# A message's scaling moved from VectorE to ScalarE and its constant to GpSimd, in the third edge stage of a four-layer graph network

## The chip, the cores and the metric

One core of a Trainium2 chip runs the whole program. The metric is device time in microseconds. The kernel before took 4991.14 us, the median of three runs (4990.61 to 4994.25).

## The reference, cut to what matters

The network has 3125 nodes, 103125 edges sorted by destination, and 64 features. Each of its four layers reads `h`, the rectified layer norm of the node rows, and adds its result to them. The change is in the third layer only, in the work done once per edge:

```python
def _mlp(x, ln_w, ln_b, W, b):
    h = _layer_norm(x, ln_w, ln_b)
    h = h @ W.T + b
    return leaky_relu(h, 0.01)
hn = _mlp(node_z, ...)            # 32 features per node
he = _mlp(edge_z, ...)            # 32 features per edge
msg = concatenate([hn[src], he])  # 64 features per edge
emb_edge = _mlp(msg, red_ln_w, red_ln_b, red_W, red_b)
msg_sum = segment_sum(emb_edge, dst) + emb_local
z = msg_sum / (deg + 1)
```

The layer norm's mean and weights are folded into the matrices beforehand. What is left per edge of the last `_mlp` is: multiply `msg` by two matrices (one gives the centred row, whose squares give the variance, the other gives the product), divide the product by the standard deviation, add the constant row `rc`, and take max(0.01 x, x). The division is a multiplication by a reciprocal, one number per edge. These three last steps are what the change redistributes.

## The kernel before, in words

Edges go in tiles of 128, one per partition, and eight tiles make a batch: there are 101 batches. Engines run their own in-order instruction lists and meet at semaphores. In `edge2` the batches come in groups of four; `q` and `h` give the place in the group (place = 2q + h, from 0 to 3). I call the stage's group "four places", and n the number of a batch, from 1.

Where the source rows `hn[src]` come from depends on the place. For places 0, 1 and 2 GpSimd gathers them with eight indirect DMAs per batch, one per tile (L950, in `Gather.gather`). For place 3 (`TAKEN`) there is no gather: TensorE picks the rows by 13 one-hot matmuls twice (`choose`, L1803), from one-hot matrices that VectorE writes (`hot`, L1947, 13 per group), and VectorE multiplies the outcome by a mask in two halves (`take`, L1957).

The order of the work of batch n is written out by hand on each engine:

- VectorE: `edge_row(n)` (L1963 to L1973: reciprocal, scale, constant, leaky relu of the edge part, which waits for ScalarE's `std1_ready`), the one-hot matrix of batch n-1 (L982), at place 3 the first `take`, then `add(n-2)`, eight additions to the accumulator (L1997) with up to five `hot` between them, at place 3 the second `take`, and last `message(n-1)`: reciprocal (L1979), scaling of eight tiles from PSUM (L1981), constant (L1984), leaky relu (L1987).
- TensorE: transposes of batch n (L1840; at place 3 L1812 and L1814), the edge matmuls of batch n+1 (L1787), then, after ScalarE has copied the transposes and VectorE has read the previous product (`u_sc`), the message matmuls of n (L1856), at place 2 the first `choose`, and the sums by destination of batch n-1 (L1795).
- ScalarE: copy of the transposes of n (L1899), eight squares and a root for the edge part of n+1 (L1876, L1880, `std1_ready`), the same for the message of n (`std2_ready`).
- GpSimd: the gathers, four batches ahead of their use. Besides waiting for the index list and for the buffer to be free, each half batch (four gathers) has a wait of its own in `midway`: at place 0 the second half waits for the sums of batch n-5, at place 1 the first half for the message matmuls of n-4 and the second for the transposes of n-3, at place 2 for sums of n-5 and message matmuls of n-3, n being the batch gathered.
- SyncE starts the loads of index lists, edge attributes and source numbers.

The buffers `u` and `u2` are single; the message product `rp`, in PSUM, is single too.

Of the kernel before, what the change touches and what calls it, by code (L numbers as in the profile page):

```python
# [203 lines left out]
def over(ap, n):  # L204

    return ap.unsqueeze(2).to_broadcast([ap.shape[0], ap.shape[1], n])
# [1471 lines left out]
def edge2(nc, k, cat, ga, catTp_ready):  # L1678


    with Ctx(nc, "edge2_") as c:
# [40 lines left out]
        by_bank = catTp[:, :, :].rearrange("p i e -> p (i e)")  # L1722
        row, ec, rc = fixed[:, 0:P].unsqueeze(1), fixed[:, P:P + HALF], fixed[:, 2 * P:2 * P + D]

        with nc.Block() as block:
# [37 lines left out]
            @block.gpsimd  # L1763
            def _(pool):
                def midway(pool, t, h, q, m, j):
                    if h == 1:
                        if j == 0:
# [7 lines left out]
                    elif q == 1:  # L1775
                        wait_past(pool, rp_ready, GROUP * (m - 1) + 4)
                ga.loop(nc, pool, begun=True, midway=midway)

# [93 lines left out]
            def _(act):  # L1872
# [17 lines left out]
                for i in (0, 1):  # L1890
                    act.activation(parts[:, :, i, 0, :], hn[:, i, :, :], ACT.Copy).then_inc(high_ready, 1)

                def body(t, first, last):
                    for h in (0, 1):
                        if empty(last, h):
                            continue
                        n = 2 * t + h + 1
                        act.wait_ge(catTp_ready, n + 2)
                        act.activation(catT[:, :, :], catTp[:, :, :], ACT.Copy).then_inc(catT_ready, 1)  # L1899
                        if not empty(last, h + 1):  # L1900
                            act.wait_ge(hep_ready, n + 1)
                            root(hep[:, :, HALF:HALF + D], 0, n + 1, sq1, std1_ready)
                        act.wait_ge(rp_ready, n)
                        root(rp[:, :, D:2 * D], 1, n, sq2, std2_ready)
                ends_apart(act, body)

            @block.vector
            def _(dve):
# [3 lines left out]
                dve.tensor_copy(ec, k.ec[:, :]).then_inc(row_ready, 1)  # L1912
                dve.tensor_copy(rc, k.rc[:, :]).then_inc(row_ready, 1)
                dve.memset(msg[0][:, :, D], 1.0)
                dve.memset(msg[1][:, :, D], 1.0).then_inc(ones_ready, 1)

                dve.wait_ge(row_ready, 3)
                step = Chain(dve, prep)
# [57 lines left out]

                def message(n, h):
                    dve.wait_ge(std2_ready, n)
                    dve.reciprocal(st[:, 5, :], st[:, 4, :]).then_inc(inv2, 1)  # L1979
                    dve.wait_ge(inv2, n)  # L1980
                    dve.tensor_tensor(u[:, :, :], rp[:, :, 0:D], over(st[:, 5, :], D),  # L1981
                                      ALU.mult).then_inc(u_sc, 1)
                    dve.wait_ge(u_sc, n)
                    dve.tensor_tensor(u2[:, :, :], u[:, :, :], rows_over(rc, B),  # L1984
                                      ALU.add).then_inc(u_b, 1)
                    dve.wait_ge(u_b, n)
# [27 lines left out]
                def body(t, q, m):  # L2014
                    first = isinstance(t, int) and t == 0
                    for h in (0, 1):
# [7 lines left out]
                        if b == TAKEN:  # L2024
                            take(m, 0)
                        if not first:
                            add(n - 2, h, t - 1, m + (b == TAKEN), due(t, m, b))
# [5 lines left out]
                        if not (first and h == 0):  # L2033
                            message(n - 1, 1 - h)
                by_parity(dve, body)
                onehot(dve, k, oh[0][:, :, :], PAIRS - 1, 0, row).then_inc(oh_ready, 1)
                add(USED - 1, 1, PAIRS - 2)
                message(USED, 0)
                add(USED, 0, PAIRS - 1)

# [766 lines left out]
```

## Time and profile before

| what | value |
|---|---|
| median of three runs | 4991.14 us |
| profiled execution, first to last instruction | 5820.0 us |
| profiled execution's own time beyond that span | none is given |
| stage of the change in it (first to last instruction, about) | 2520 to 3660 us |
| its steady part that is read below | 2560 to 3640 us |
| mean granted TensorE clock, whole span / steady part | 0.875 / 0.85 |

The profiled execution is 829 us, or 16.6%, longer than the median of the runs. The table of stretches in the rows below cuts the program into its parts (three edge stages, then the fourth edge stage in two passes, with short node stages between them); the line of the stage of the change is shown. A stretch's line gives the busy time of each engine with its number of instructions. An engine's time between instructions is given in the groups as idle time with what ended it.

### The profile page before, as it was taken

Reading aid. Unit: us, or ns where it says so; the run is one execution under the profiler, and the core shown is the slowest. Engines: PE = TensorE matmul, PEld = TensorE weight load, DVE = VectorE, ACT = ScalarE, POOL = GpSimd, SP = SyncE. Lnnn points to the kernel's source line nnn. Section 1 sums busy time; section 2 is a strip of 40 time slices with the busy share of each in tenths; the row PEclk is TensorE's granted clock in tenths of the full one; section 3 lists DMA queues with packets and bytes.
Section 4 is the critical chain, followed back from the end, with each engine's and each line's share of the span. In section 5 each row is a group of like instructions: output and inputs, shape, how many; then the busy total and the mean of one; then the engine's idle time right before and its main releaser. Section 6 shows DMA issues by size and latency. Waiting matters only on the chain. (4 is left out here: it accounts for less than half of the span.)

```text
span 5820.0 us, 104938 instructions
## 1 busy us (share of the span) xinstructions
PE 4388.1 (75%) x29528; PEld 2834.6 (49%) x29528; DVE 4126.9 (71%) x7954; ACT 2011.5 (35%) x6556; POOL 3270.2 (56%) x2950
## 2 busy tenths in 40 slices
PE   2999899989677777756777777376777667549998
PEld 1444444444344444445555555244444434349998
DVE  4767676766777676767777777466666666789998
ACT  2656566666000000134434444000000000057775
POOL 4666666663566666455555554455555555325554
PEclk6999999999788888778888888688888888779998
DMA  4333333331212111121111111233333333211111
GB/s 114 91 90 94 87 87 93 94 87 48 52 43 44 40 43 44 23 47 45 45 42 47 44 45 35 63 101 103 100 103 101 105 106 102 78 43 47 49 49 33
DMA packets 493105, 394.00 MB, mean 68 GB/s; under 512 B 346007, under 2 KB 379168, under 8 KB 492904
## 3 DMA queue, kind: packets, MB, share of 16 engines
q1 hardware_dynamic: 395496, 303.53, 18.3%
q0 software_dynamic: 90560, 83.37, 8.0%
q10 hardware_dynamic: 6976, 6.23, 0.3%
q8 instruction: 34, 0.56, 0.0%
q14 instruction: 39, 0.32, 0.0%
HBM read 355.34 MB, written 37.42 MB: 67 GB/s over the span
## 5 line engine op out<-in xcount | busy, mean ns | idle before, releaser
L1093 POOL DMA_INDIRECT edge_src_rows<-table_wh,edge_gather_idx x806 | 867.8, 1077 | 503.0 <-issue 229.7
L950 POOL DMA_INDIRECT edge3a_src_rows<-table_h,edge3a_gather_idx x808 | 763.1, 944 | 632.7 <-issue 259.0
L2165 PE MATMUL edge3a_z_ps<-Wz,edge3a_both_ends_t 128*128 128x396 f32 x1616 | 736.3, 600 | 405.0 <-DVE edge3a_terms L2258 322.0
L1123 PE MATMUL edge_sums_ps<-edge_onehot_src,edge_halves 128*128 128x512 bf16 x4840 | 890.0, 331 | 43.2 <-issue 32.4
L950 POOL DMA_INDIRECT table_cat<-table_hn,table_gather_idx x592 | 624.9, 1056 | 479.6 <-PE edge_sums_ps L1795 181.2
L1508 POOL DMA_INDIRECT edge_src_rows<-table_h,edge_gather_idx x608 | 609.1, 1002 | 424.4 <-issue 175.4
L2258 DVE SCALAR_TENSOR_TENSOR edge3a_terms<-edge3a_z_ps,att_z 128x792 f32<-128x792 f32 x404 | 386.1, 977 | 486.6 <-DMA edge_edge_attr<-in_ea 307.5
L2165 PEld LDWEIGHTS edge3a_z_ps<-Wz,edge3a_both_ends_t 128*128 128x128 f32 x1616 | 346.6, 226 | 733.7 <-DVE edge3a_terms L2258 368.3
L1123 PEld LDWEIGHTS edge_sums_ps<-edge_onehot_src,edge_halves 128*128 128x128 f16 x4840 | 385.6, 97 | 477.4 <-issue 69.5
L2577 PE MATMUL edge3b_sums_ps<-edge3b_onehot,edge3b_weighted 128*128 128x128 f32 x4848 | 572.9, 279 | 6.3 <-DVE layers_accT L2615 4.4
L2577 PEld LDWEIGHTS edge3b_sums_ps<-edge3b_onehot,edge3b_weighted 128*128 128x128 f32 x4848 | 553.6, 193 | 12.0 <-DVE layers_accT L2615 4.6
L2494 POOL TENSOR_TENSOR edge3b_weighted<-edge3b_src_rows,edge3b_alpha 128x1920 f32<-128x1920 f32 x101 | 350.2, 3468 | 345.4 <-DVE edge3b_alpha L2594 251.4
L2204 ACT ACTIVATE edge3a_both_ends_t<-edge3a_both_ends_t_ps 128x1024 f32<-128x1024 f32 x101 | 103.4, 1024 | 1245.3 <-DMA edge_edge_attr<-in_ea 992.0
L2543 ACT ACTIVATE edge3b_weighted<-edge3b_src_rows,edge3b_alpha 128x64 f32<-128x64 f32 x1818 | 445.2, 334 | 166.2 <-DVE edge3b_alpha L2594 157.4
L1523 PE MATMUL edge_src_rows_t_ps<-edge_onehot_src,edge_h_halves 128*128 128x512 f16 x1300 | 364.2, 415 | 142.3 <-DVE edge_onehot_src L1629 75.3
L1211 DVE TENSOR_SCALAR edge_onehot_src<-layer_node_row,edge_src_col,edge_magnitude 128x1568 bf16<-128x1568 f16 x605 | 416.9, 690 | 26.0 <-remote 18.1
L1301 DVE TENSOR_TENSOR edge_halves<-edge_weighted_ps,edge_halves 128x512 f16<-128x512 f32 x204 | 131.0, 683 | 345.9 <-ACT edge_halves L1172 266.7
L2266 DVE TENSOR_REDUCE edge3a_scores<-edge3a_terms 128x24 f32<-128x1584 f32 x202 | 364.5, 1805 | 6.9
L1123 PE MATMUL edge_sums_ps<-edge_onehot_src_act,edge_halves 128*128 128x512 bf16 x1608 | 307.3, 330 | 60.2 <-issue 40.0
L1164 ACT ACTIVATE edge_onehot_src_act<-edge_distance,edge_magnitude,edge_minus_magnitude 128x1568 bf16<-128x1568 f16 x201 | 340.5, 1694 | 10.5
L1629 DVE TENSOR_SCALAR edge_onehot_src<-edge_src_everywhere,node_col 128x1024 f16<-128x1024 f16 x650 | 333.0, 516 | 9.2
L1593 ACT ACTIVATE edge_msg<-edge_msg_ps 128x512 f32<-128x512 f32 x101 | 60.3, 597 | 791.2 <-remote 451.6
(370 smaller groups left out, 7950.6 us busy)
## 6 DMA issues: line engine op xcount, KB each, us to landing
edge_dst_row<-in_dst_row SPq DMA_DIRECT2D x102, 512.0 KB
edge3a_dst_row<-in_dst_row SPq DMA_DIRECT2D x102, 512.0 KB
edge_window<-table_wh_parts SPq DMA_DIRECT2D x816, 48.8 KB
edge3a_window<-table_h SPq DMA_DIRECT2D x816, 32.0 KB
edge_edge_attr<-in_ea SPq DMA_DIRECT2D x101, 256.0 KB
kept_rows<-edge3a_src_rows SPq DMA_DIRECT2D x101, 256.0 KB
edge3b_src_rows<-kept_rows SPq DMA_DIRECT2D x101, 256.0 KB
edge_edge_attr<-in_ea SPq DMA_DIRECT2D x101, 128.0 KB
```

The source lines that it names most:

```text
L950: nc.gpsimd.indirect_dma_start(self.slot(b, j), None, self.table[:, :], bass.IndirectOffsetOnAxis(ap=self.idx[b][:, j:j + 1], axis=0)).the ...
L1093: nc.gpsimd.indirect_dma_start(g[q][:, j, :], None, k.t_wh[:, :], bass.IndirectOffsetOnAxis(ap=idx[q][:, j:j + 1], axis=0)).then_inc(gathe ...
L1123: mm = pe.matmul(acc[:, i, 0:w], halves[q][:, j, a, :, :].rearrange("p h d -> p (h d)"), hot[:, o:o + w], start=first and a == 0, stop=False)
L1211: dve.tensor_scalar(slot_v(q, j)[:, :], k.node_row[:, :], col[q][:, j:j + 1], mag[q][:, j:j + 1], ALU.is_equal, ALU.mult).then_inc(hot_v, 1)
L1508: nc.gpsimd.indirect_dma_start(g[p][:, j, :], None, k.t_h[:, :], bass.IndirectOffsetOnAxis(ap=idx[p][:, j:j + 1], axis=0)).then_inc(gather ...
L1523: mm = pe.matmul(rowsTp[:, o:o + 512], h16[:, b, :], ring[b % RING][:, o:o + 512], start=(b == 0), stop=(b == NB - 1))
L2165: mm = pe.matmul(zp[q % 2][:, i, 0:H * ZH], hcT[h][:, j * P:(j + 1) * P], k.Wz[:, :], start=True, stop=True)
L2258: dve.scalar_tensor_tensor(terms[:, 2 * q:2 * q + 2, :], zp[q % 2][:, :, 0:H * ZH], 0.0, rows_over(k.att_z[:, :], 2), ALU.max, ALU.mult).t ...
L2266: dve.tensor_reduce(scs[h][:, :, j:j + B // 2].rearrange("p h b -> p b h"), terms[:, j:j + B // 2, :].rearrange("p b (h f) -> p b h f", h= ...
L2494: return engine.tensor_tensor(hp[h][:, a:b, :, :], rows, weights, ALU.mult)
L2543: w = act.activation(hp[h][:, j, a, :], st[h][:, j, :], ACT.Copy, scale=al[h][:, a, j:j + 1])
L2577: mm = pe.matmul(sums[j % 4][:, i, :], hp[h][:, j, 2 * i:2 * i + 2, :].rearrange("p a d -> p (a d)"), oh[h][:, j, :], start=True, stop=True)
```

## The change

VectorE keeps the reciprocal (`invert`) and the leaky relu (`finish`). The reciprocal now comes before `add`, and the leaky relu stays where `message` was. ScalarE scales the product tile by tile, eight activations of 128x64 from PSUM with the reciprocal as scale, at the head of the next batch's body, ahead of the copy of the transposes. GpSimd adds the constant row with one operation of 128x512, read from SBUF: at places 0 to 2 in the middle of a batch's eight gathers, ahead of the second half's own wait, at place 3 by itself. The constant's copy in PSUM goes.

```diff
             @block.gpsimd
+                def shift(n):
+                    pool.wait_ge(u_sc, n)
+                    nc.gpsimd.tensor_tensor(u2[:, :, :], u[:, :, :], rows_over(k.rc[:, :], B),
+                                            ALU.add).then_inc(u_b, 1)
                 def midway(pool, t, h, q, m, j):
+                    if j and live_shift(t, h):
+                        shift(2 * t + h - 3)
                     if h == 1:
...
-                ga.loop(nc, pool, begun=True, midway=midway)
+                def live_shift(t, h):
+                    return not isinstance(t, int) or 2 * t + h >= 4
+                def body(t, q, m):
+                    if isinstance(t, int) and t == 0:
+                        return
+                    for h in (0, 1):
+                        if not used_batch(t, h):
+                            continue
+                        ga.gather(nc, pool, t, h, q, m, midway=midway)
+                        if 2 * q + h == TAKEN and live_shift(t, h):
+                            shift(2 * t + h - 3)
+                by_parity(pool, body)
+                for n in range(USED - 3, USED + 1):
+                    shift(n)
             @block.scalar
+                def scale(n):
+                    act.wait_ge(inv2, n)
+                    wait_past(act, u_b, n - 1)
+                    for j in range(B):
+                        a = act.activation(u[:, j, :], rp[:, j, 0:D], ACT.Copy, scale=st[:, 5, j:j + 1])
+                    a.then_inc(u_sc, 1)
                 def body(t, first, last):
                         n = 2 * t + h + 1
+                        if not (first and h == 0):
+                            scale(n - 1)
                         act.wait_ge(catTp_ready, n + 2)
...
+                scale(USED)
             @block.vector
-                dve.tensor_copy(rc, k.rc[:, :]).then_inc(row_ready, 1)
...
-                def message(n, h):
+                def invert(n):
                     dve.wait_ge(std2_ready, n)
                     dve.reciprocal(st[:, 5, :], st[:, 4, :]).then_inc(inv2, 1)
-                    dve.wait_ge(inv2, n)
-                    dve.tensor_tensor(u[:, :, :], rp[:, :, 0:D], over(st[:, 5, :], D),
-                                      ALU.mult).then_inc(u_sc, 1)
-                    dve.wait_ge(u_sc, n)
-                    dve.tensor_tensor(u2[:, :, :], u[:, :, :], rows_over(rc, B),
-                                      ALU.add).then_inc(u_b, 1)
+                def finish(n, h):
                     dve.wait_ge(u_b, n)
                     dve.scalar_tensor_tensor(msg[h][:, :, 0:D], u2[:, :, :], 0.01, u2[:, :, :],
                                              ALU.mult, ALU.max).then_inc(msg_ready, 1)
...
+                        if not (first and h == 0):
+                            invert(n - 1)
                         if not first:
                             add(n - 2, h, t - 1, m + (b == TAKEN), due(t, m, b))
...
-                            message(n - 1, 1 - h)
+                            finish(n - 1, 1 - h)
```

## Rows read from the trace of the kernel before

**Rows 1.** The head of the profile's page: span, then busy time of each engine.

```profile
span 5820.0 us, 104938 instructions
## 1 busy us (share of the span) xinstructions
PE 4388.1 (75%) x29528; PEld 2834.6 (49%) x29528; DVE 4126.9 (71%) x7954; ACT 2011.5 (35%) x6556; POOL 3270.2 (56%) x2950
```

**Rows 2.** The table of stretches, the line of this stage; columns head it.

```profile
core 0: us, PE busy (x) PEld busy (x) DVE busy (x) ACT busy (x) POOL busy (x), PEclk, DMA share, GB/s
...
2520.00:3660.00 1140.00, 790.62 (x6056) 611.09 (x6056) 826.78 (x2208) 465.13 (x3538) 624.92 (x592) 0.84 0.18 44
```

**Rows 3.** The scalings' line: count, shortest/median/longest ns, first and last start.

```profile
L1981 DVE TENSOR_TENSOR edge_u<-edge_msg_ps,edge_stat x101: 690/692/693, 2547.8 to 3651.8; 128x512 f32<-128x512 f32 x101
```

**Rows 4.** The same table for the stage's steady part alone.

```profile
2560.00:3640.00 1080.00, 760.86 (x5852) 585.94 (x5853) 790.56 (x2110) 447.19 (x3417) 602.54 (x569) 0.85 0.18 43
```

**Rows 5.** Who waited for whom in the steady part: us in total, times, longest.

```profile
ACT edge_squares L1876 <- DMA edge_edge_attr<-in_ea: 215.6, 38, 9.4
DVE edge_stat L1963 <- ACT edge_stat L1880: 182.1, 57, 8.5
...
PE edge_msg_ps L1856 <- DVE edge_u L1981: 165.0, 55, 4.6
```

**Rows 6.** VectorE in order of time, one group: start, length, [idle before].

```profile
2787.10 0.20 DVE L1963 RECIPROCAL edge_stat<-edge_stat 128x8 f32<-128x8 f32 x1 [8.24 <-ACT edge_stat L1880]
...
2790.96 0.62 DVE L1947 TENSOR_SCALAR edge_onehot_src<-edge_src_in_half,edge_node_no 128x1024 f16<-128x1024 f16 x1 [0.29 <-PE edge_cat_t_ps L1803]
...
2798.98 0.20 DVE L1963 RECIPROCAL edge_stat<-edge_stat 128x8 f32<-128x8 f32 x1 [1.91 <-ACT edge_stat L1880]
...
2801.67 0.28 DVE L1997 TENSOR_TENSOR layers_accT<-layers_accT,edge_sums_ps 65x128 f32 x1
...
2809.74 0.20 DVE L1963 RECIPROCAL edge_stat<-edge_stat 128x8 f32<-128x8 f32 x1 [2.11 <-ACT edge_stat L1880]
...
2817.92 0.20 DVE L1963 RECIPROCAL edge_stat<-edge_stat 128x8 f32<-128x8 f32 x1
...
2824.69 0.69 DVE L1987 SCALAR_TENSOR_TENSOR edge_msg<-edge_u 128x512 f32<-128x512 f32 x1
2833.11 0.20 DVE L1963 RECIPROCAL edge_stat<-edge_stat 128x8 f32<-128x8 f32 x1 [7.72 <-ACT edge_stat L1880]
```

**Rows 7.** TensorE in order of time, third batch of that group.

```profile
2821.64 1.14 PE L1787 MATMUL edge_he_ps<-eR,edge_edge_attr 64*128 64x96 f32 x16
```

**Rows 8.** ScalarE in order of time, third batch of that group.

```profile
2830.99 0.22 ACT L1876 ACTIVATE edge_squares<-edge_he_ps 128x64 f32<-128x64 f32 x1 [8.03 <-DMA edge_edge_attr<-in_ea]
...
2832.77 0.30 ACT L1880 ACTIVATE edge_stat<-edge_stat,eps 128x8 f32<-128x8 f32 x1
```

**Rows 9.** Groups of instructions of VectorE, steady part, shapes apart; columns head it.

```profile
line engine op names shapes xcount | busy us, mean ns | idle before us <-releasers
...
L1987 DVE SCALAR_TENSOR_TENSOR edge_msg<-edge_u 128x512 f32<-128x512 f32 x97 | 67.5, 695 | 3.4
L1981 DVE TENSOR_TENSOR edge_u<-edge_msg_ps,edge_stat 128x512 f32<-128x512 f32 x97 | 67.1, 692 | 3.3
L1984 DVE TENSOR_TENSOR edge_u<-edge_u,edge_constants_ps 128x512 f32<-128x512 f32 x97 | 66.6, 686 | 3.3
...
L1979 DVE RECIPROCAL edge_stat<-edge_stat 128x8 f32<-128x8 f32 x97 | 18.5, 191 | 0.0
```

**Rows 10.** Groups of ScalarE in the second pass of the fourth stage.

```profile
L2543 ACT ACTIVATE edge3b_weighted<-edge3b_src_rows,edge3b_alpha 128x64 f32<-128x64 f32 x1818 | 445.2, 334 | 166.2 <-DVE edge3b_alpha L2594 157.4 <-DMA edge3b_src_rows<-kept_rows 8.8
```

**Rows 11.** Groups of ScalarE in the steady part.

```profile
L1899 ACT ACTIVATE edge_cat_t<-edge_cat_t_ps 128x512 f32<-128x512 f32 x97 | 57.5, 593 | 255.1 <-PE edge_cat_t_ps L1814 122.6 <-issue 79.8 <-DMA edge_gather_idx<-in_src_t 35.3
```

**Rows 12.** GpSimd's groups over the whole span.

```profile
L950 POOL DMA_INDIRECT edge3a_src_rows<-table_h,edge3a_gather_idx x808 | 763.1, 944 | 632.7 <-issue 259.0 <-DMA kept_rows<-edge3a_src_rows 165.5 <-DMA edge_edge_attr<-in_ea 137.7
...
L2494 POOL TENSOR_TENSOR edge3b_weighted<-edge3b_src_rows,edge3b_alpha 128x1920 f32<-128x1920 f32 x101 | 350.2, 3468 | 345.4 <-DVE edge3b_alpha L2594 251.4 <-DMA edge3b_src_rows<-kept_rows 94.0
...
L854 POOL TENSOR_TENSOR node_heads<-layers_accT,layer_accT 128x256 f32<-128x256 f32 x1 | 2.4, 2426 | 0.0
```

**Rows 13.** GpSimd's groups in the steady part.

```profile
L950 POOL DMA_INDIRECT table_cat<-table_hn,table_gather_idx x569 | 602.5, 1059 | 458.2 <-PE edge_sums_ps L1795 181.2 <-issue 153.2 <-PE edge_msg_ps L1856 106.7
```

**Rows 14.** GpSimd's waits in the steady part: us in total, times, longest.

```profile
POOL table_cat L950 <- PE edge_sums_ps L1795: 181.2, 47, 7.7
POOL table_cat L950 <- issue: 153.2, 470, 2.0
POOL table_cat L950 <- PE edge_msg_ps L1856: 106.7, 41, 8.3
```

**Rows 15.** GpSimd in order of time, two gathers of the group above.

```profile
2790.39 0.94 POOL L950 DMA_INDIRECT table_cat<-table_hn,table_gather_idx  x1 [6.97 <-PE edge_sums_ps L1795]
2791.64 1.98 POOL L950 DMA_INDIRECT table_cat<-table_hn,table_gather_idx  x1 [0.30 <-issue]
```

More of the change, by code:

```diff
@@ L1722, in edge2 @@
         by_bank = catTp[:, :, :].rearrange("p i e -> p (i e)")
-        row, ec, rc = fixed[:, 0:P].unsqueeze(1), fixed[:, P:P + HALF], fixed[:, 2 * P:2 * P + D]
+        row, ec = fixed[:, 0:P].unsqueeze(1), fixed[:, P:P + HALF]
         with nc.Block() as block:
@@ L1912, in _ @@
                 dve.tensor_copy(ec, k.ec[:, :]).then_inc(row_ready, 1)
-                dve.tensor_copy(rc, k.rc[:, :]).then_inc(row_ready, 1)
                 dve.memset(msg[0][:, :, D], 1.0)
                 dve.memset(msg[1][:, :, D], 1.0).then_inc(ones_ready, 1)
-                dve.wait_ge(row_ready, 3)
+                dve.wait_ge(row_ready, 2)
                 step = Chain(dve, prep)
@@ L2033, in body @@
                         if not (first and h == 0):
-                            message(n - 1, 1 - h)
+                            finish(n - 1, 1 - h)
                 by_parity(dve, body)
                 onehot(dve, k, oh[0][:, :, :], PAIRS - 1, 0, row).then_inc(oh_ready, 1)
+                invert(USED)
                 add(USED - 1, 1, PAIRS - 2)
-                message(USED, 0)
+                finish(USED, 0)
                 add(USED, 0, PAIRS - 1)
```

## The prediction

> **What bounds the kernel now.** I read the head of the page, the table of stretches, the waits of the stage, and one group of four batches in order of time. The page says that no engine is full: TensorE is busy 75%, VectorE 71%, GpSimd 56% [rows 1]. The table of stretches puts the stage of the change at 2520 to 3660 us [rows 2]; 101 batches in it are 25.25 groups, and I use 1105 us for them, from the first scaling at 2547.8 to the last at 3651.8 [rows 3], or 43.8 us a group. In its steady part VectorE is busy 790.6 of 1080 us, GpSimd 602.5, ScalarE 447.2 [rows 4].
>
> The waits are where the reader must be careful. ScalarE waits 215.6 us for something to square, and VectorE 182.1 us for ScalarE's root [rows 5]. In the group in order of time VectorE starts batches at 2787.10, 2798.98, 2809.74, 2817.92 and 2833.11, so places 3, 0, 1 and 2 take 11.88, 10.76, 8.18 and 15.19 us [rows 6]. The 15.19 hold an idle time of 7.72. TensorE's record of the matmuls that ScalarE needs next ends at 2821.64 + 1.14 = 2822.78 [rows 7]; ScalarE starts on them at 2830.99, having been idle 8.03 [rows 8]. The records show nothing in those eight microseconds that it needed. The same, smaller, lies before 2809.74. I take these two pauses as belonging to the profiled execution only, because that execution is 829 us longer than the median of the runs (5820.0 [rows 1] against 4991.14) and the time must be somewhere. That is a choice, and a rival below drops it.
>
> Without them a group takes 11.88 + (10.76 - 2.11) + 8.18 + (15.19 - 7.72) = 36.2 us [rows 6], 914 us for the stage. In 36.2 us VectorE idles only some 2 or 3: in the timed runs **VectorE's order bounds the stage now**, at place 3 joined by TensorE's picking.
>
> **What the change does, part by part.** My sum is for one group, times 25.25. It is made on the records of the profiled execution less the two pauses, and its difference is then added to the median of 4991.14.
>
> *VectorE, removed.* Scaling and constant, 0.692 and 0.686 us each as single instructions [rows 9], follow each other every 0.72: 1.44 us a batch. At places 0 to 2 this is on the path; at place 3 VectorE idles 1.91 us afterwards for ScalarE [rows 6], and it is hidden. VectorE alone would then need 8.65 - 1.44 = 7.2, 6.7 and 6.0 us there. The one reciprocal is moved, not removed: 0.19 us [rows 9]. The copy of the constant at the start is 64 columns, once: nothing.
>
> *TensorE, a wait shortened.* The message matmuls wait for the scaling in 55 batches, 165.0 us [rows 5], since `add` stood before it. That wait now ends earlier. What is late next is ScalarE's copy of the transposes.
>
> *ScalarE, added.* Eight activations a batch with a scale of one number per partition. The like row is that of 128x64 activations with such a scale: 445.2 us for 1818, 0.245 each, 0.334 for a lone one [rows 10]. So 7 x 0.245 + 0.334 = 2.05 us. The source is PSUM there and SBUF in the row; the squares read PSUM and come no slower. Bounds: 1.6 us (the step of the squares without that scale: 2830.99 to 2832.77 is 1.78 with the last one's end [rows 8]) and 8 x 0.334 = 2.7. ScalarE is busy 447.2 of 1080 [rows 4], so it has the time, but its place is at the head of the body, and what is queued behind it is the copy, the squares and the root that VectorE's next batch waits for. This makes a loop. From VectorE's first reciprocal of a batch: edge part and one-hot matrix to 2801.67, 2.69 us after 2798.98 [rows 6]; reciprocal and handing over 0.24; scaling 2.05; copy 0.59 [rows 11] and handing over 0.06; squares and root, from the first square to VectorE's next reciprocal, 2833.11 - 2830.99 = 2.12 [rows 6, 8]. Sum 7.75. So places 0 to 2 cannot fall to VectorE's 7.2, 6.7 and 6.0, but to 7.75 each; place 2 even grows from 7.47. Place 3 stays at 11.88, its scaling lying beside TensorE's picking. A group by this loop: 3 x 7.75 + 11.88 = 35.1.
>
> *GpSimd, added.* One addition of 128x512 a batch. The nearest like row is the 128x1920 product, 3.468 us [rows 12]; in proportion 0.925, and I take 1.0, and 0.1 for starting it. Below, 0.93; above, the 128x256 addition of the last node stage, 2.43 [rows 12], which reads with a permuted step, so that I hold it for the far end. GpSimd's own work: 24 gathers a group, mean 1.059 us [rows 13], each with a gap of 153.2 / 470 = 0.326 [rows 14]: 24 x 1.385 = 33.2 us. With four additions, 33.2 + 4 x 1.1 = **37.6 us**. This is more than the 36.2 of now and the 35.1 of ScalarE's loop.
>
> Its slack is what pays today: it waits 181.2 and 106.7 us for TensorE [rows 14], most of it in the profiled pauses. Without them it has 36.2 - 33.2 = 3.0 us a group, and gets 4.4 of work. *The wait added:* `shift` waits for ScalarE's scaling; queued behind it are the second half of a batch's gathers and all later ones; TensorE's transposes four batches on wait for these. And the other way: VectorE's `finish`, and behind it the next edge part, wait for the addition; so does ScalarE's next scaling, since `u` is single, and behind that the copy and the root. GpSimd running late thus stops all four engines. SyncE's index loads wait for the gathers, as before, one group ahead.
>
> *Two rules weighed.* The trace's gathers take 0.944 in the first pass of the fourth stage [rows 12] and 1.059 here [rows 13]; one that started at 2791.64 took 1.98 while VectorE wrote one-hot matrices [rows 6, 15]. The Trainium skill (SBUF — State Buffer, Who interferes with whom) says that VectorE's fast two-port operations and GpSimd exclude each other for a whole instruction. By that rule, which these rows agree with, an addition that meets `hot` costs one of the two up to the other's length; at 0.3 us a meeting it would be four times 0.3, 1.2 us a group, 30 us more. No row shows an addition meeting one, and it is not in my sum. The Trainium skill (GPSIMD Engine Reference, Performance versus the Vector engine) gives some 2.6 cycles an element for a two-input addition and advises VectorE for it; an estimate from that page is 1.1 us for 512 elements beside the row's 0.925, 10 us more over the stage.
>
> **The sum.** 37.6 - 36.2 = +1.4 us a group, x 25.25 = +35. Start and end of the stage add a last addition and its handing over, 1 us. 4991 + 36 = **5027 us**, slower by 0.7%.
>
> **Rivals.**
>
> *GpSimd does not bind; the kernel gets faster.* If the 0.326 gap between gathers is partly the profiler's, GpSimd's 37.6 shrinks: it decides below a gap of (35.1 - 4.4 - 24 x 1.059) / 24 = 0.22. Then the group is ScalarE's 35.1: -1.1 x 25.25 = -28, **4963 us**. For it: the whole execution is slowed by profiling. Against it: the gap is the same 0.30 in all gathers, whatever surrounds them. Chance 0.18.
>
> *The two pauses are real.* Then GpSimd has 43.8 - 37.6 = 6 us to spare. Place 1 goes from 8.18 to 7.75, place 2 in the groups without a pause does not gain, and what TensorE's shortened wait gives is at most the 1.44 us of place 0: 0.4 to 1.8 a group, 10 to 45 us, **4970 us**. For it: nothing in the records separates a real wait from a profiled one. Against it: the 829 us. Chance 0.10.
>
> *The addition's wait stops the gathers.* At place 0 the second half waited for sums that were there; now it waits for the scaling, ready 2.69 + 0.24 + 2.05 = 5.0 us into the next batch, while the first half (4 x 1.385 = 5.5 us, started with the transposes at 2.3) ends at 7.8, the batch's own end. So up to 5.0 us of idle a group where GpSimd is on time, none where it is late by them. As it binds, I take half: 2.5 x 25.25 = +63 on top, **5090 us**; an addition of 1.7 us in place of 1.0 gives the same. Chance 0.22.
>
> *The edits cancel*: GpSimd's 37.6 overlaps the slow places so that 36.2 stays, within 10 us of **4991**. Chance 0.14.
>
> My forecast has 0.36. This kernel's measurement tells 0.2%, 10 us, from no change. Faster: 0.18 + 0.10 = 0.28. Same: 0.14. Slower: 0.36 + 0.22 = 0.58. The range goes from 4950, which takes in both faster rivals' values, to 5100; the forecast's own is 5005 to 5050. The far ends of the addition's price (2.43 us: +1.4 x 101 = 141 more) lie outside.
>
> **What would show it.** After, the addition's group should say about 1.0 us x 101; the scaling's 808 activations 0.25 each. GpSimd's waits for TensorE should be nearly gone in unpaused groups, with short ones for ScalarE's scaling in their place, and VectorE should wait for GpSimd before L1987's successor, which it never does now. TensorE's 165.0 us for L1981 should have no successor of that size. The profiled span may even shrink where the pauses remain, since there GpSimd has room; the timed median is what my sum is about. I am wrong if GpSimd still idles 2 us or more a group in unpaused groups, if the addition takes over 1.5 us, or if the stage gets shorter in the timed runs.

## The result, and the profile after

The changed kernel takes **5033.26 us** (median, 5029.01 to 5033.79), the kernel before 4990.88 in runs beside it (4988.85 to 4994.25): slower by 0.81%, ratio 1.0081, 95% interval 1.0068 to 1.0094. The forecast was 5027.

The head of the page after, as [rows 1]:

```profile
span 5031.9 us, 105710 instructions
## 1 busy us (share of the span) xinstructions
PE 4094.4 (81%) x29353; PEld 2742.8 (55%) x29528; DVE 4021.6 (80%) x7751; ACT 2176.0 (43%) x7364; POOL 3411.7 (68%) x3051
```

The span is 5031.9 us, beside runs of 5033: this profile shows the kernel as it runs when timed. That of [rows 1] did not (5820.0 beside 4991), so the kernel before was profiled once more. From here "before" means that second profile (it stands as an experiment below), and group lengths are counted as the first to the last batch of the stage over 25 groups of four batches.

The stretch from 2300 to 3150 us, first after and then before, columns as in [rows 2]:

```profile
2300.00:3150.00 850.00, 622.78 (x5192) 482.25 (x5191) 612.01 (x1709) 531.94 (x3706) 680.95 (x605) 0.90 0.22 50
```

```profile
2300.00:3150.00 850.00, 647.55 (x5431) 522.38 (x5432) 736.99 (x1975) 420.77 (x3177) 571.27 (x537) 0.87 0.21 51
```

VectorE lost 125 us of work in the same 850 us, GpSimd got 110 more. The granted TensorE clock of this stretch is 0.90 after and 0.87 before, so the loss is not a lower clock. Next the one-line summaries (count; shortest, median, longest ns; first and last start), of the new addition and scaling after, and of the old scaling before, which answers to [rows 3]:

```profile
L1767 POOL TENSOR_TENSOR edge_u<-edge_u,rc x101: 1260/1274/1668, 2223.4 to 3200.8; 128x512 f32<-128x512 f32 x101
```

```profile
L1919 ACT ACTIVATE edge_u<-edge_msg_ps,edge_stat x808: 304/328/360, 2221.6 to 3200.4; 128x64 f32<-128x64 f32 x162
```

```profile
L1981 DVE TENSOR_TENSOR edge_u<-edge_msg_ps,edge_stat x101: 690/692/692, 2236.0 to 3170.0; 128x512 f32<-128x512 f32 x101
```

The addition and the old scaling each come once a batch, so their first and last starts give the stage: 977.4 us after, 934.0 before, **39.1 and 37.4 us a group**. The stage's 43 us are the whole loss of 42. (The profiled spans differ by 31 only: the second profile of the kernel before took 5002 us, 11 more than its median, and its stage starts 14 us later, at 2236.0 against 2221.6.)

GpSimd's groups after (busy us, mean ns, idle before and its releasers), as [rows 13]:

```profile
L950 POOL DMA_INDIRECT table_cat<-table_hn,table_gather_idx x519 | 567.8, 1094 | 147.7 <-issue 143.8 <-PE edge_sums_ps L1817 2.7 <-PE edge_msg_ps L1878 0.3
L1767 POOL TENSOR_TENSOR edge_u<-edge_u,rc 128x512 f32<-128x512 f32 x86 | 113.7, 1323 | 21.6 <-ACT edge_u L1919 20.5
```

Add up: 567.8 + 113.7 busy, 143.8 of the fixed gaps between gathers, 23.5 of all waits, together 849 of 850 us. GpSimd had 115 us of waits for TensorE in the kernel before and has 3.0 now; it never rests. That it sets the pace is what the experiments test. One group is 24 x (1.094 + 143.8 / 519) + 4 x 1.323 = 32.9 + 5.3 = 38.2, plus waits of 0.9 for ScalarE's scaling: 39.1, the measured length.

The waits after on VectorE, as [rows 5] (total, times, longest):

```profile
DVE edge_msg L2014 <- POOL edge_u L1767: 214.6, 53, 6.1
...
DVE edge_stat L1994 <- ACT edge_stat L1902: 4.1, 9, 1.0
```

VectorE now waits 214.6 us for GpSimd's addition, a wait that did not exist, and hardly at all for ScalarE's root (4.1 us). TensorE's wait for the scaling (165.0 us in [rows 5]) has no successor; in its place stands what was named as late next, ScalarE's copy:

```profile
PE edge_msg_ps L1878 <- ACT edge_cat_t L1930: 79.8, 68, 1.9
```

How the addition arrives late is seen in one group in order of time (start, length, [idle before]), first GpSimd, as [rows 15]:

```profile
2578.12 1.64 POOL L1767 TENSOR_TENSOR edge_u<-edge_u,rc 128x512 f32<-128x512 f32 x1 [1.15 <-ACT edge_u L1919]
2579.91 1.41 POOL L950 DMA_INDIRECT table_cat<-table_hn,table_gather_idx  x1
...
2589.11 0.94 POOL L950 DMA_INDIRECT table_cat<-table_hn,table_gather_idx  x1 [0.30 <-issue]
2590.07 1.27 POOL L1767 TENSOR_TENSOR edge_u<-edge_u,rc 128x512 f32<-128x512 f32 x1
2591.50 1.40 POOL L950 DMA_INDIRECT table_cat<-table_hn,table_gather_idx  x1 [0.16 <-issue]
...
2602.70 1.27 POOL L1767 TENSOR_TENSOR edge_u<-edge_u,rc 128x512 f32<-128x512 f32 x1
...
2608.42 1.98 POOL L950 DMA_INDIRECT table_cat<-table_hn,table_gather_idx  x1 [0.30 <-issue]
2610.42 1.27 POOL L1767 TENSOR_TENSOR edge_u<-edge_u,rc 128x512 f32<-128x512 f32 x1
...
2617.86 1.60 POOL L1767 TENSOR_TENSOR edge_u<-edge_u,rc 128x512 f32<-128x512 f32 x1 [0.52 <-ACT edge_u L1919]
```

and VectorE, as [rows 6]:

```profile
2578.15 0.48 DVE L1978 TENSOR_SCALAR edge_onehot_src<-edge_src_in_half,edge_node_no 128x1024 f16<-128x1024 f16 x1
...
2579.80 0.69 DVE L2014 SCALAR_TENSOR_TENSOR edge_msg<-edge_u 128x512 f32<-128x512 f32 x1 [0.34 <-POOL edge_u L1767]
...
2583.52 0.20 DVE L2010 RECIPROCAL edge_stat<-edge_stat 128x8 f32<-128x8 f32 x1
...
2591.38 0.69 DVE L2014 SCALAR_TENSOR_TENSOR edge_msg<-edge_u 128x512 f32<-128x512 f32 x1 [5.82 <-POOL edge_u L1767]
...
2604.00 0.69 DVE L2014 SCALAR_TENSOR_TENSOR edge_msg<-edge_u 128x512 f32<-128x512 f32 x1 [4.46 <-POOL edge_u L1767]
...
2609.66 0.47 DVE L1978 TENSOR_SCALAR edge_onehot_src<-edge_src_in_half,edge_node_no 128x1024 f16<-128x1024 f16 x1
...
2610.26 1.72 DVE L1978 TENSOR_SCALAR edge_onehot_src<-edge_src_in_half,edge_node_no 128x1024 f16<-128x1024 f16 x1
...
2612.52 0.68 DVE L2014 SCALAR_TENSOR_TENSOR edge_msg<-edge_u 128x512 f32<-128x512 f32 x1
```

and ScalarE's eight scalings between them, merged into one line:

```profile
2583.83 1.75 ACT L1919 ACTIVATE edge_u<-edge_msg_ps,edge_stat 128x64 f32<-128x64 f32 x8 [1.07 <-DVE edge_stat L2010]
```

VectorE hands over its reciprocal at 2583.72 (2583.52 + 0.20), and ScalarE has scaled by 2585.58. GpSimd starts the addition only at 2590.07, 4.5 us later, since it stands behind eight gathers that began at 2579.91. VectorE gets its message at 2591.38 after 5.82 us of idling. The second thing to see is at 2610: a one-hot write that takes 0.47 us takes 1.72 when it meets the addition of 2610.42, and the addition of 2578.12 takes 1.64 instead of 1.27 beside the write of 2578.15. The two hold each other up.

VectorE's one-hot writes after and before (columns as in [rows 9]):

```profile
L1978 DVE TENSOR_SCALAR edge_onehot_src<-edge_src_in_half,edge_node_no 128x1024 f16<-128x1024 f16 x281 | 172.6, 614 | 4.9 <-PE edge_cat_t_ps L1825 4.9
```

```profile
L1947 DVE TENSOR_SCALAR edge_onehot_src<-edge_src_in_half,edge_node_no 128x1024 f16<-128x1024 f16 x293 | 139.0, 474 | 0.0
```

Their mean went from 474 to 614 ns: 13 writes a group (293 in 850 us), 1.8 us.

### The profile page after: what moved, and what is told of

Read it like the earlier page. It is cut to its first block and busy times, and to the rows that moved or that the text cites. A ratio compares the mean times of both kernels' runs of the same rounds, so it can differ in the third digit from the quotient of the medians.

```text
span 5031.9 us, 105710 instructions
## 1 busy us (share of the span) xinstructions
PE 4094.4 (81%) x29353; PEld 2742.8 (55%) x29528; DVE 4021.6 (80%) x7751; ACT 2176.0 (43%) x7364; POOL 3411.7 (68%) x3051
## 5 line engine op out<-in xcount | busy, mean ns | idle before, releaser
L1093 POOL DMA_INDIRECT edge_src_rows<-table_wh,edge_gather_idx x806 | 852.0, 1057 | 332.8 <-issue 255.2
L1123 PE MATMUL edge_sums_ps<-edge_onehot_src,edge_halves 128*128 128x512 bf16 (+1 forms) x4689 | 857.3, 327 | 23.1 <-DVE edge_onehot_src L1211 14.6
L950 POOL DMA_INDIRECT table_cat<-table_hn,table_gather_idx x592 | 647.0, 1093 | 180.3 <-issue 164.8
L2195 PE MATMUL edge3a_z_ps<-Wz,edge3a_both_ends_t 128*128 128x396 f32 x1616 | 583.3, 512 | 10.1 <-DVE edge3a_terms L2288 8.5
L2573 ACT ACTIVATE edge3b_weighted<-edge3b_src_rows,edge3b_alpha 128x64 f32<-128x64 f32 x1818 | 445.2, 334 | 165.5 <-DVE edge3b_alpha L2624 156.6
L2195 PEld LDWEIGHTS edge3a_z_ps<-Wz,edge3a_both_ends_t 128*128 128x128 f32 x1616 | 292.9, 191 | 257.0 <-DVE edge3a_terms L2288 76.9
L2186 PE MATMUL edge3a_both_ends_t_ps<-edge3a_onehot_t,edge3a_window 128*64 128x128 f32 x1616 | 223.7, 298 | 213.6 <-DMA edge3a_src_rows<-table_h,edge3a_gather_idx 213.4
L1817 PE MATMUL edge_sums_ps<-edge_onehot,edge_msg 128*65 128x128 f32 x1616 | 246.7, 318 | 140.3 <-issue 77.8
L2186 PEld LDWEIGHTS edge3a_both_ends_t_ps<-edge3a_onehot_t,edge3a_window 128*64 128x64 f32 x1616 | 198.2, 150 | 275.2 <-issue 178.3
```

What stands on the lines that cost most here:

```text
L950: nc.gpsimd.indirect_dma_start(self.slot(b, j), None, self.table[:, :], bass.IndirectOffsetOnAxis(ap=self.idx[b][:, j:j + 1], axis=0)).the ...
L1093: nc.gpsimd.indirect_dma_start(g[q][:, j, :], None, k.t_wh[:, :], bass.IndirectOffsetOnAxis(ap=idx[q][:, j:j + 1], axis=0)).then_inc(gathe ...
L1123: mm = pe.matmul(acc[:, i, 0:w], halves[q][:, j, a, :, :].rearrange("p h d -> p (h d)"), hot[:, o:o + w], start=first and a == 0, stop=False)
L2186: pe.matmul(hcTp[D:P, cols], win[h][:, j, :], oht[h][:, cols], start=True, stop=True)
L2195: mm = pe.matmul(zp[q % 2][:, i, 0:H * ZH], hcT[h][:, j * P:(j + 1) * P], k.Wz[:, :], start=True, stop=True)
L2573: w = act.activation(hp[h][:, j, a, :], st[h][:, j, :], ACT.Copy, scale=al[h][:, a, j:j + 1])
```

## The experiments

All ratios are to the kernel before, in runs on the same chip, with 95% intervals (its medians there lie between 4990 and 4995 us); "group" is the stage's length per four batches. Diffs are against the changed kernel.

**The kernel before, once more** (no edit). It was to say whether the two pauses in [rows 6] are the kernel's.

> The kernel before, profiled once more. The profile of the changed kernel spans 5031.9 us and its median is 5033.3, so that execution shows nearly the timed run; the one of before spans 5820.0 against 4991. If the pauses of 2.1 and 7.7 us in a group belong to that one profiled execution, this profile spans about 4990, a group of four batches takes 36 to 37 us (the prediction's 36.2), VectorE idles 2 to 3 us in it, and GpSimd waits 3 to 4 us in it. If they are real, the span is again above 5400 and a group takes 43 to 44.

One run took 5002.31 us, the profiled span is 5000.5, the group 37.4. The waits:

```profile
PE edge_msg_ps L1856 <- DVE edge_u L1981: 169.3, 67, 3.9
POOL table_cat L950 <- issue: 143.9, 439, 1.5
...
POOL table_cat L950 <- PE edge_sums_ps L1795: 81.1, 35, 3.0
...
DVE edge_stat L1963 <- ACT edge_stat L1880: 44.7, 27, 1.9
DVE layers_accT L1997 <- PE edge_sums_ps L1795: 43.3, 52, 0.9
POOL table_cat L950 <- PE edge_msg_ps L1856: 34.3, 35, 1.6
```

VectorE's wait for the root fell from 182.1 us, longest 8.5, to 44.7, longest 1.9. The pauses are not in the kernel; the choice to take them out was right. The other expectations were missed a little: a group takes 37.4 us and not 36 to 37, VectorE waits 88 us for others (3.9 a group, not 2 to 3), and GpSimd 115 (5.1 a group, not 3 to 4). VectorE is busy 737 of 850 us: its order is read as the bound.

**The constant back on VectorE** (const_on_vector). The scaling stays on ScalarE; GpSimd gets nothing.

```diff
                 def shift(n):
-                    pool.wait_ge(u_sc, n)
-                    nc.gpsimd.tensor_tensor(u2[:, :, :], u[:, :, :], rows_over(k.rc[:, :], B),
-                                            ALU.add).then_inc(u_b, 1)
+                    pass
...
                 def finish(n, h):
+                    dve.wait_ge(u_sc, n)
+                    dve.tensor_tensor(u2[:, :, :], u[:, :, :], rows_over(rc, B),
+                                      ALU.add).then_inc(u_b, 1)
```

> The changed kernel, with the constant added by VectorE again (before the leaky relu, 0.69 us a batch), ScalarE's scaling kept where it is. Theory (GpSimd's list is full: 24 gathers of 1.37 us and four additions of 1.32, 38.2 of the 39.3 us that a group takes): GpSimd has 33 us of work again and stops binding; the places 0 to 2 take VectorE's 7.9, or ScalarE's loop of 7.75, and a group 35 to 36 us: 4960 to 4985 us, under both kernels. Rival (ScalarE's scaling ahead of the copy is what made it slower): the loop is unchanged, and so is the time, 5020 to 5035.

4953.34 us, ratio 0.9917 (0.9904 to 0.993), group 35.7; 7 us under the expected range. The half of the change that goes to ScalarE is worth 40 us (4993.37 for the kernel before beside it); the half that goes to GpSimd costs 80 on top of it. The one-hot writes are back at 486 ns. The ScalarE half also puts the reciprocal ahead of `add`, and no run moves VectorE's own scaling there with the constant left on VectorE; so how much of the 40 us is the engine and how much the earlier place is open.

**The scaling back on VectorE** (scale_on_vector). The other half alone; `scale` goes from ScalarE's body (not shown).

```diff
                 def invert(n):
                     dve.reciprocal(st[:, 5, :], st[:, 4, :]).then_inc(inv2, 1)
+                    dve.wait_ge(inv2, n)
+                    wait_past(dve, u_b, n - 1)
+                    dve.tensor_tensor(u[:, :, :], rp[:, :, 0:D], over(st[:, 5, :], D),
+                                      ALU.mult).then_inc(u_sc, 1)
```

> The changed kernel with the scaling done by VectorE in one operation, right behind its reciprocal and ahead of the additions to the accumulator; the constant stays on GpSimd. ScalarE is as before the change. Theory (GpSimd's list is full): the same 38.2 us of GpSimd's work in a group, so 5020 to 5040 us, no faster than the changed kernel by more than 10. Rival (ScalarE's loop): it is gone, VectorE has 0.69 us less than before the change on its path, and the time falls under 4985.

5045.4 us, 1.0103 (1.0088 to 1.0117), group 39.5; 5 us over the expected range. GpSimd's constant alone costs 52 us, all of the loss and more. Its groups:

```profile
L950 POOL DMA_INDIRECT table_cat<-table_hn,table_gather_idx x511 | 548.7, 1074 | 161.2 <-issue 136.1 <-PE edge_msg_ps L1878 22.9
L1767 POOL TENSOR_TENSOR edge_u<-edge_u,rc 128x512 f32<-128x512 f32 x85 | 108.2, 1273 | 32.6 <-DVE edge_u L2010 31.6
```

24 x (1.074 + 0.266) + 4 x 1.273 is 37.3, and its waits of 54.5 us in 21.5 groups are 2.5: 39.8, near the measured 39.5. These waits are longer than the changed kernel's 0.9.

**The addition twice** (double_addition), the first time into a buffer that nobody reads, to price one addition.

```diff
+                    nc.gpsimd.tensor_tensor(u3[:, :, :], u[:, :, :], rows_over(k.rc[:, :], B), ALU.add)
                     nc.gpsimd.tensor_tensor(u2[:, :, :], u[:, :, :], rows_over(k.rc[:, :], B),
```

> The changed kernel, with GpSimd's addition done twice a batch, the first into a buffer that nobody reads. Theory (GpSimd's list is full, so each microsecond on it is one of the stage's): 101 more additions of 1.32 us are 133 us, so 5033 + 133 = 5166, between 5150 and 5185. Rival (it is the places of the waits that cost, GpSimd has slack): well under that, below 5120.

5157.75 us, 1.0332 (1.0316 to 1.0348), group 44.0. That is 124 us over the changed kernel, for 101 additions of 1.30 = 131: nearly each microsecond given to GpSimd lengthens the kernel.

**Two columns of 64** (two_columns): the wait and its place stay, the work all but goes.

```diff
-                    nc.gpsimd.tensor_tensor(u2[:, :, :], u[:, :, :], rows_over(k.rc[:, :], B),
+                    nc.gpsimd.tensor_tensor(u2[:, :, 0:2], u[:, :, 0:2], rows_over(k.rc[:, 0:2], B),
...
+                dve.memset(u2[:, :, :], 0.0)
```

> The changed kernel with all its waits, but GpSimd adds the constant to 2 of 64 columns of each tile alone, the others of the buffer being zero from the start: 128x16 in place of 128x512. Theory (the length of the addition fills GpSimd's list): four additions of about 0.2 in place of 1.32 us leave 34 us of GpSimd's work in a group; VectorE stops waiting for it and the time falls to 4950 to 4985. Rival (it is the place of the additions: each stands behind up to eight gathers, and each stops the gathers behind it until ScalarE has scaled): the waits stay, and the time stays above 5015.

4958.7 us, 0.9921 (0.9901 to 0.9941). The six runs lie apart, three from 4942 to 4948 and three from 4970 to 4975; the profile, with a group of 36.6, is of the longest.

```profile
L1767 POOL TENSOR_TENSOR edge_u<-edge_u,rc x101: 215/228/689, 2229.1 to 3143.3; 128x16 f32<-128x16 f32 x101
```

The addition takes 0.228 us (median; mean 0.297 in the 850 us). 75 us are gone by the medians, 58 to 91 by single runs, though VectorE still waits 130.6 us for GpSimd (46 times, longest 4.1) behind the gathers: the work on GpSimd's list is most of the loss, and it was wrong to expect VectorE's waits to end. VectorE has one instruction of 0.69 less a batch than in const_on_vector (4953), and by the medians is no faster. That the late arrival eats this saving fits the waits, but the spread of the runs is too wide to show it.

**The scaling behind ScalarE's copy** (scale_behind_copy), in the changed kernel.

```diff
-                        if not (first and h == 0):
-                            scale(n - 1)
                         act.wait_ge(catTp_ready, n + 2)
                         act.activation(catT[:, :, :], catTp[:, :, :], ACT.Copy).then_inc(catT_ready, 1)
+                        if not (first and h == 0):
+                            scale(n - 1)
```

> The changed kernel, with ScalarE's scaling behind its copy of the transposes and ahead of the squares. Theory (GpSimd's list is full): ScalarE's order decides nothing, 5025 to 5045. Rival (ScalarE's loop has a share): 10 us or more either way.

5088.51 us, 1.0193 (1.0178 to 1.0209), group 41.0: no change was expected, and it is 55 us slower than the changed kernel. The waits:

```profile
DVE edge_msg L2014 <- POOL edge_u L1767: 276.9, 82, 6.5
ACT edge_cat_t L1928 <- PE edge_cat_t_ps L1836: 243.2, 20, 13.3
...
PE edge_msg_ps L1878 <- ACT edge_u L1919: 132.5, 83, 2.4
```

At place 3 the copy waits for TensorE's picking, up to 13.3 us; the scaling is now queued behind that, and GpSimd and VectorE behind the scaling. GpSimd waits 54.4 us in 20.7 groups, 2.6 a group in place of 0.9.

**The same order, with the constant on VectorE** (const_on_vector_copy_first), the edits of const_on_vector and scale_behind_copy together.

> The kernel with the constant on VectorE and the scaling on ScalarE (4953 us), with the scaling behind the copy of the transposes. There GpSimd does not bind; the loop over ScalarE's list and VectorE's own list are within 0.2 us a batch of each other. The loop has the same length in either order if the copy does not wait, and gains up to the copy's 0.6 us where the copy was ready and the reciprocal was not: TensorE waits 100.7 us for the copy there. If the loop binds places 0 to 2: 4925 to 4945. If VectorE's own list binds: 4945 to 4960.

4993.37 us, 1.0 (0.9991 to 1.0009), group 37.4: 40 us over const_on_vector, and outside both expected ranges. The same cause (the copy waits 182.3 us, longest 9.2; VectorE 92.6 us for the scaling) without GpSimd in it. The place of the scaling at the head of the body, which the prediction took as given, is needed for the whole gain of ScalarE's half.

**The constant on GpSimd for place 3's message alone** (const_split): const_on_vector with one batch in four on GpSimd.

```diff
-                def finish(n, h):
+                def finish(n, h, by_pool=False):
+                    if not by_pool:
+                        dve.wait_ge(u_sc, n)
+                        dve.tensor_tensor(u2[:, :, :], u[:, :, :], rows_over(rc, B),
+                                          ALU.add).then_inc(u_b, 1)
...
-                            finish(n - 1, 1 - h)
+                            finish(n - 1, 1 - h, b == 0)
```

> The kernel with scaling on ScalarE, the constant on VectorE at three places of four, and on GpSimd for the message of place 3, where GpSimd has no gather. GpSimd then has 33 + 1.3 = 34.3 us of work in a group of 35.7. If a place on the list is all that counts, VectorE gains 0.69 us in one batch of four: 17 us, 4936. If the addition, met by VectorE's writing of one-hot matrices, makes these wait, the gain is lost: 4950 to 4965.

4976.23 us, 0.9964 (0.9951 to 0.9978), group 36.5: 23 us worse than leaving it on VectorE, and over both expected ranges. VectorE waits 1.5 us in all for GpSimd, so it is not lateness. It is mostly the one-hot writes, VectorE's line in this kernel:

```profile
L1976 DVE TENSOR_SCALAR edge_onehot_src<-edge_src_in_half,edge_node_no 128x1024 f16<-128x1024 f16 x290 | 170.4, 587 | 0.0
```

587 ns against 486: 13 x 0.10 = 1.3 us a group, for 0.69 saved, a net 0.6 of the 0.8 that a group grew. Place by place the traces agree: place 0, where the addition falls, takes 8.50 us against 7.97 in const_on_vector, its five writes 3.77 against 2.51; the other 0.2 us lies at place 3 and is open.

**The same where no one-hot write runs** (const_split_quiet): place 1's message, finished in place 2's body; `b == 0` above becomes `b == 2`, and GpSimd's addition stands in place 1's second half.

> As the split kernel (4976 us), but the message whose constant GpSimd adds is that of place 1, which VectorE finishes in the body of place 2, where it writes no one-hot matrices for the picking. In the split kernel these writes rose from 0.486 to 0.587 us, 13 of them 1.3 us a group, more than the 0.69 that VectorE saves. Theory (the addition on GpSimd and VectorE's two-speed writes shut each other out): the mean write stays at 0.49, VectorE's 0.69 stay saved, and the time comes under the 4953 of the kernel with the constant on VectorE, or within 5 us of it, for the body of place 2 is bound by ScalarE's loop: 4935 to 4960. Rival (any addition on GpSimd costs by the wait behind its four gathers): 4970 or more.

4973.82 us, 0.9958 (0.9945 to 0.9971), group 36.6. The writes are back at 487 ns, as expected, and yet nothing is gained: the time is in the rival's range, not the theory's; GpSimd and VectorE in order of time:

```profile
2600.57 0.94 POOL L950 DMA_INDIRECT table_cat<-table_hn,table_gather_idx  x1 [0.30 <-issue]
2601.54 1.27 POOL L1767 TENSOR_TENSOR edge_u<-edge_u,rc 128x512 f32<-128x512 f32 x1
2602.97 1.40 POOL L950 DMA_INDIRECT table_cat<-table_hn,table_gather_idx  x1 [0.16 <-issue]
```

```profile
2597.67 0.20 DVE L2008 RECIPROCAL edge_stat<-edge_stat 128x8 f32<-128x8 f32 x1
...
2602.85 0.69 DVE L2016 SCALAR_TENSOR_TENSOR edge_msg<-edge_u 128x512 f32<-128x512 f32 x1 [3.13 <-POOL edge_u L1767]
```

The addition comes 3.7 us after the reciprocal's end, behind the gathers that stand ahead of it, and VectorE idles 3.13 for it (75.4 us, 23 times). Place 2, where this falls, takes 8.66 us against 7.25 in const_on_vector, and place 3 gets back 0.7 of it. So one cost was exchanged for the other, and both are seen in the trace.

**The additions in other places** (additions_spread): in the changed kernel, behind the 4th, 10th, 16th and 22nd gather of a group.

```diff
-                    if j and live_shift(t, h):
+                    if live_shift(t, h) and (h == 0 and q == 0 and j == 4 or h == 1 and j == 2 or q == 1 and j == 0):
                         shift(2 * t + h - 3)
+                    if q == 1 and j == 6 and live_shift(t, h + 1):
+                        shift(2 * t + h - 2)
```

> The changed kernel with the four additions of a group behind the 4th, 10th, 16th and 22nd of its 24 gathers, in place of the 4th, 12th, 20th and 24th; the gathers' own waits are where they were. GpSimd's work is the same: 24 x 1.37 + 4 x 1.32 = 38.2 us a group, of the 39.1 that a group takes. Theory (the total binds): between 38.2 and 39.1 us a group, 5010 to 5035 us. Rival (the uneven distance of the additions is most of the loss: VectorE waits up to 6.1 us for the late ones): 5000 or less.

5015.65 us, 1.0041 (1.0029 to 1.0053), group 38.2.

```profile
L950 POOL DMA_INDIRECT table_cat<-table_hn,table_gather_idx x533 | 587.2, 1102 | 149.5 <-issue 149.2 <-PE edge_msg_ps L1880 0.3
L1767 POOL TENSOR_TENSOR edge_u<-edge_u,rc 128x512 f32<-128x512 f32 x89 | 113.5, 1276 | 1.6
```

GpSimd hardly waits now (0.3 us for TensorE), and its list is 24 x (1.102 + 0.280) + 4 x 1.276 = 38.3, the measured group to 0.1. The changed kernel's other 0.9 us a group is the wait for the scaling.

**The second reciprocal first** (early_inverse: the changed kernel; const_on_vector_early_inverse: with the constant on VectorE). ScalarE waited 220.6 us for that reciprocal after the change; it stood behind the one-hot matrix of 1.21 us, and at place 3 behind the first `take`.

```profile
ACT edge_u L1919 <- DVE edge_stat L2010: 220.6, 87, 5.8
```

```diff
+                            invert(n - 1)
...
-                        if not (first and h == 0):
-                            invert(n - 1)
```

> The changed kernel (constant on GpSimd) with the same single step that took 39 us off the kernel with the constant on VectorE: the reciprocal ahead of the one-hot matrix, so that ScalarE scales 0.7 us or more earlier in each batch. Theory (GpSimd's list is full): GpSimd waits for the scaling 20.5 us in 86 additions, that is all it can win: 5015 to 5033. Rival (ScalarE's loop is what binds here as well): 39 us or so off, 5000 or less.

> The kernel with the constant on VectorE and the scaling on ScalarE, and VectorE's reciprocal ahead of the one-hot matrix of the batch before. The loop by ScalarE's list, from root to root, loses the one-hot matrix's 1.13 us less a wait of some 0.4 for the second root: VectorE waits 95 us for that root now, 57 times. If the loop binds there, half or more of these go: 4900 to 4935 us. If VectorE's own list binds, the new wait costs as much as it gives: 4945 to 4965.

early_inverse takes 5006.78 us, 1.003 (1.002 to 1.0041), group 37.9. GpSimd's lines:

```profile
L950 POOL DMA_INDIRECT table_cat<-table_hn,table_gather_idx x532 | 580.5, 1091 | 149.0 <-issue 146.3 <-PE edge_cat_t_ps L1862 1.2 <-PE edge_sums_ps L1817 0.3
L1767 POOL TENSOR_TENSOR edge_u<-edge_u,rc 128x512 f32<-128x512 f32 x89 | 113.8, 1278 | 4.2 <-ACT edge_u L1919 1.9
```

Its wait for the scaling goes from 20.5 to 1.9 us, the additions' mean from 1.323 to 1.278; the list is 24 x (1.091 + 146.3 / 532) + 4 x 1.278 = 37.9, again the measured group. The gain of 26 us is more than the wait that was to be all it could win, and the time is 8 us under the expected range: of the 1.2 us a group, 0.9 is the wait, 0.2 the additions and 0.1 the gathers. **const_on_vector_early_inverse takes 4914.62 us**, 0.9836 (0.9823 to 0.9849), group 34.1, and beats both kernels. The same edit is worth 26 us where GpSimd is the bound and 39 where it is not.

## Why the prediction was right

*What bounds before.* Right: VectorE's order. The group was put at 36.2 us from the records less the pauses, and is 37.4; VectorE idles 88 us of 850 for ScalarE's root and TensorE's sums, 3.9 a group, where "some 2 or 3" had been read. From the first scaling to the last are 25 groups, not 25.25; this is worth 0.4 us in the 43.8, and nothing in the forecast.

*VectorE and TensorE.* As described: 1.44 us a batch gone, and ScalarE's copy late next.

*ScalarE.* The size of one term was off: eight scalings take 1.75 us, not 2.05. The loop's 35.1 us a group cannot be seen alone; const_on_vector, where VectorE keeps 0.69 us a batch, has 35.7. In the changed kernel it does not bind. What the loop's reading did not see is that one part of it could go: the 1.2 us that the reciprocal stands behind the one-hot matrix.

*GpSimd.* The step that carried the forecast, and it is shown: a list of 24 gathers and four additions that sets the pace (double_addition lengthens the kernel by nearly what it adds, and the list's sum is the measured group in additions_spread and early_inverse). Forecast 33.2 + 4.4 = 37.6; measured 32.9 for the gathers, 5.3 for the additions, 0.9 of waits, 39.1. The mis-sized term is the addition, 1.323 us on average where 1.0 and a start of 0.1 had been taken from the 128x1920 product in proportion to its columns [rows 12]. The estimate from the Trainium skill (GPSIMD Engine Reference, Performance versus the Vector engine), 1.1 us, was nearer than the row's 0.925, and its advice to leave such an addition to VectorE is borne out: const_on_vector is 80 us faster than the changed kernel.

*The difference.* Forecast +1.4 us a group, measured 39.1 - 37.4 = +1.7, times 25: +43, against +35. Both lengths had been read too short, by 1.5 and 1.2; most of the two errors cancel, and 5027 against 5033 looks better than its terms. Part of this is luck. In the kernel before GpSimd's list is 24 x (1.064 + 143.9 / 537) = 32.0 us, so its slack was 5.4 and not 3.0; what came on top was 5.3 of additions, 0.9 of dearer gathers and 0.9 of waits, 7.1 and not 4.4.

*The rule that was left out of the sum.* The Trainium skill (SBUF — State Buffer, Who interferes with whom) has VectorE's two-port operations and GpSimd exclude each other. The trace after agrees: 0.47 becomes 1.72 us beside an addition, the mean 474 becomes 614 ns. In the changed kernel this falls on VectorE, which waits anyway. What shows of it in the additions on GpSimd's list is their mean of 1.323 against a median of 1.274, 0.2 us a group, where the prediction weighed 1.2; of the 0.9 us of dearer gathers about half comes from another meeting, told in the last section. Where VectorE is the bound, it decides (const_split: 1.3 us a group).

*The rivals.* "GpSimd does not bind" fell: the gap is 0.30 in the undisturbed profiles too. Its 4963 us is near what the kernel has without the addition's work on GpSimd (const_on_vector 4953, two_columns 4959). "The pauses are real" fell with before_again. "The addition's wait stops the gathers" was true in kind and dear by less: 0.9 us a group instead of 2.5; early_inverse takes it away. "The edits cancel" fell.

## What to carry to other kernels

Before work goes to an engine that looks idle, write down its whole list for one period, fixed gaps included: at 32 us of 37.4 it was full but for its waits for others, and four additions of 1.3 made it the bound. A queue in order has a second price, lateness: an operation of 1.3 us behind eight gathers of 1.25 each started 4.5 us after its input was ready, and the engine that needed it waited up to 6.1. Of a change in two halves run each by itself; here one gained 40 us by itself and the other cost 52, and 80 on top of the first. And look at what follows the moved work: as large a gain (39 us) was one reciprocal issued some 1.2 us earlier, once GpSimd was not the bound.

## What was not expected of the hardware

- A profiled execution can differ much from the timed ones: 5820.0 us and then 5000.5 for the same kernel, with idle times up to 8 us in the first that are missing from the second. What held TensorE's signal back in the first is open.
- The 128x512 addition takes 1.274 us (median), 128x16 takes 0.228: (1274 - 228) / 496 = 2.11 ns a column. The 128x1920 product takes 3.468 [rows 12], and by the same start (3468 - 228) / 1904 = 1.70. Which of operands and shape makes the difference was not tried.
- VectorE's leaky relu holds up a gather that starts just behind it. The gathers of 2579.91 and 2591.50 above take 1.41 and 1.40 us instead of 0.94, and each starts 0.12 us after a leaky relu (2579.80, 2591.38). It is not the addition ahead of them: in the kernel before, without any addition, the gather of 2602.96 takes 1.30 beside the leaky relu of 2602.75, and in const_split, where the leaky relu comes later, the 21 gathers behind an addition take 0.97. But the addition is what releases the leaky relu, and so it lines the two up. The gathers' mean is 1.094 after, 1.064 before and 1.048 in const_on_vector.

```profile
2602.96 1.30 POOL L950 DMA_INDIRECT table_cat<-table_hn,table_gather_idx  x1 [0.30 <-issue]
```

```profile
2602.75 0.69 DVE L1987 SCALAR_TENSOR_TENSOR edge_msg<-edge_u 128x512 f32<-128x512 f32 x1
```

- Eight 128x64 activations with a scale per partition end in 1.75 us from PSUM, (1.75 - 0.33) / 7 = 0.20 apart. In [rows 10], which read SBUF, 18 in a row take 445.2 / 101 = 4.41, (4.41 - 0.33) / 17 = 0.24 apart. Only these two rows speak for it.
